# Perceiver attention block on one core: scores in four row tiles of 32 partitions instead of two of 64, with three rotating PSUM banks instead of five

## What is computed

```
x = x + xattn(layernorm(x), ctx)    # x [8, 64, 256]; ctx [8, 1601, 256]; 16 heads of 16
x = x + causal self attention(layernorm(x))
x = x + top-2 of 8 experts(layernorm(x))             # 256 -> 1024 -> 256, exact gelu

xattn:  k = ctx @ Wk.T + bk;  v = ctx @ Wv.T + bv;  q = norm @ Wq.T + bq
        attn = softmax(q . k / 4)                     # per head, over the 1601 keys
        out  = (attn @ v) @ Wo.T + bo
```

## Time and profile before

| | us |
|---|---|
| median of 3 runs | 750.23 (747.94 to 752.42) |
| the profiled execution | 751.15 |
| its span | 749.1 |
| PE busy / DVE busy / ACT busy / POOL busy | 683.8 / 499.6 / 326.5 / 224.6 |
| matmul instructions | 6584 |
| granted TensorE clock, mean | 0.949 |

### The profile page before, as it was taken

The page is one execution under the profiler, slowest core; times in us unless marked ns, Lnnn a source line. Parts: engine busy times, 40 slices in busy tenths (PEclk is TensorE's granted clock), DMA queues, the critical chain, the costliest instruction groups (busy, mean ns, idle before and its releaser), DMA issues.

```text
span 749.1 us, 16666 instructions
## 1 busy us (share of the span) xinstructions
PE 683.8 (91%) x6584; PEld 551.7 (74%) x6584; DVE 499.6 (67%) x868; ACT 326.5 (44%) x517; POOL 224.6 (30%) x111
## 2 busy tenths in 40 slices
PE   2979999999999977999997999978787999999997
PEld 2657877778867855886775787656666999999996
DVE  4783697796658773666768657476466766766753
ACT  2434465554454542445454443345225544444431
POOL 1004566665445542535454545200000000000000
PEclk9987999999999986999998999897798999999999
DMA  6120020010010110001001000020500222112000
GB/s 221 59 67 2 23 67 24 24 46 23 24 46 4 40 49 3 24 24 45 3 23 45 1 2 2 1 114 1 225 1 1 113 113 112 32 83 112 0 0 28
DMA packets 12501, 34.16 MB, mean 46 GB/s; under 512 B 1483, under 2 KB 9812, under 8 KB 10260
## 3 DMA queue, kind: packets, MB, share of 16 engines
q1 hardware_dynamic: 12180, 31.62, 12.4%
q0 software_dynamic: 256, 1.58, 0.6%
HBM read 32.67 MB, written 0.52 MB: 44 GB/s over the span
## 4 chain that ended last, share of the span: by engine, by line
PE 79%; DVE 13%; issue 3%; ACT 2%; DMA 1%; SPq 0%; DVEq 0%; POOL 0%; ACTq 0%
PE bank L1016 44%; PE bank L1180 13%; PE bank L1025 8%; PE bank L1076 5%; DVE maxes L763 3%; DVE ctx_lo L704 2%; PE bank L1119 2%; PE bank L1110 2%; DMA bias_sb<-in_biases 1%; PE bank L1094 1%; ACT probs L639 1%; DVE qbd_hi L736 1%; DVE prob_sum L431 1%; DVE ties L811 1%; DVE shift L722 1%
## 5 line engine op out<-in xcount | busy, mean ns | idle before, releaser
L431 POOL TENSOR_TENSOR prob_sum<-probs,prob_sum 128x1024 f32<-128x1024 f32 x84 | 201.8, 2402 | 162.6 <-ACT probs L639 161.6
L763 DVE TENSOR_REDUCE maxes<-bank 128x1 f32<-128x400 f32 (+1 forms) x256 | 132.5, 567 | 33.2 <-PE bank L1076 30.6
L639 ACT ACTIVATE probs<-bank 128x1024 f32<-128x1024 f32 (+1 forms) x104 | 106.6, 1025 | 98.0 <-PE bank L1180 94.8
L621 ACT ACTIVATE h_raw<-bank,b_sb 128x512 f32<-128x512 f32 (+1 forms) x72 | 46.2, 642 | 105.6 <-PE bank L1016 105.6
L544 ACT ACTIVATE v_sb<-bank 128x256 f32<-128x256 f32 (+1 forms) x104 | 39.9, 384 | 104.5 <-PE bank L1016 104.2
L745 DVE SCALAR_TENSOR_TENSOR k_lo<-bank,bias_sb,k_hi 128x400 fp32r<-128x400 f32 (+2 forms) x64 | 40.6, 634 | 62.0 <-ACT k_hi L541 61.9
L1180 PE MATMUL bank<-qbd_hi,k_hi 64*128 64x256 f32 (+1 forms) x416 | 74.3, 352 | 6.7 <-ACT probs L639 3.4
L1016 PE MATMUL bank<-w_hi,h_hi 128*128 128x256 f32 x256 | 72.7, 284 | 0.2 <-DVE h_lo L963 0.2
L1016 PE MATMUL bank<-w_hi,h_lo 128*128 128x256 f32 x256 | 72.5, 283 | 0.0
L1025 PE MATMUL bank<-probs,v_sb 128*32 128x128 f32 (+1 forms) x1664 | 70.1, 288 | 2.5 <-DVE masked L712 2.0
L1016 PE MATMUL bank<-w_lo,h_hi 128*128 128x256 f32 x256 | 72.3, 283 | 0.0
(11 more groups left out here) (157 smaller groups left out, 1474.2 us busy)
## 6 DMA issues: line engine op xcount, KB each, us to landing
raw<-in_w SPq DMA_DIRECT2D x16, 1024.0 KB, 6.7
ctx_raw<-in_ctx_t SPq DMA_DIRECT2D x16, 400.0 KB, 3.5
ctx_raw<-in_ctx_t SPq DMA_DIRECT2D x8, 402.0 KB, 3.6
ctx_raw<-in_ctx_t SPq DMA_DIRECT2D x8, 399.0 KB, 3.5
w_sb<-in_w_t POOLq DMA_DIRECT2D x1, 1280.0 KB, 10.4
x_all<-in_x SPq DMA_DIRECT2D x1, 512.0 KB, 3.7
w_raw<-in_w_t SPq DMA_DIRECT2D x1, 512.0 KB, 4.7
result<-x_all SPq DMA_DIRECT2D x1, 512.0 KB, 2.7
```

Of the source, the lines that this page charges most:

```text
L431: engine.tensor_tensor(prob_sum[0:ROWS[k], :], probs[0:ROWS[k], s % 2, :], acc[0:ROWS[k]], ALU.add).then_inc(summed, 1)
L621: nc.scalar.activation(h_raw[:, c % 2, 0:width], bank[:, at, 0:width], ACT.Gelu, bias=b1_sb[:, bass.ds(e, 1), c:c + 1].rearrange("p a b -> ...
L639: nc.scalar.activation(probs[0:ROWS[k], s % 2, :].rearrange("p (g n) -> p g n", g=G), bank[0:ROWS[k], 0:ROW_TILES, :], ACT.Exp, scale=SCAL ...
L763: nc.vector.tensor_reduce(maxes[:, g * PAIRS + j, c:c + 1], src[:, 0:width], AX.X, ALU.max).then_inc(read_dve, 1)
```

## The change

Four row tiles of 32 partitions take the place of two of 64. A row tile holds two heads, so `qbd` has 2 x 64 = 128 columns per group, half of before, and its mask is the two-column parity mask that was already loaded. Each row tile writes to its own bank, so scores take four banks (256 columns of each), and the ring of units keeps three. The M units, still taken two at a time, contract over 32 partitions. The order of probabilities in `probs` changes with it, and its size does not.

```
-ROW_TILES = 2
+ROW_TILES = PAIRS
 RT = P // ROW_TILES
 RH = HG // ROW_TILES
+M_AT_ONCE = 2
...
-RING = 5
+RING = 3
...
     c, rest = divmod(u, G * PAIRS)
-    g, rest = divmod(rest, PAIRS)
-    i, r = divmod(rest, ROW_TILES)
+    g, j = divmod(rest, PAIRS)
...
-                                         bank[0:ROWS[k], 0:ROW_TILES, :], ACT.Exp,
+                                         bank[0:ROWS[k], 0:ROW_TILES, 0:G * RH * Q], ACT.Exp,
...
-                mask = row_mask[:, :].unsqueeze(1).unsqueeze(3).broadcast_to([P, G, RH, Q])
+                mask = mask_sb[:, HG:HG + RH].unsqueeze(1).unsqueeze(3).broadcast_to([P, G, RH, Q])
...
-                r, i = divmod(j, PAIRS // ROW_TILES)
-                return (r * G + g) * (PAIRS // ROW_TILES) + i
+                return j * G + g
...
-                    rows = slice(RT * r, RT * r + RT)
+                    rows = slice(RT * j, RT * j + RT)
                     ins = nc.tensor.matmul(dst[:, 0:width],
-                                           qbd_hi[rows, parity, g, 2 * i:2 * i + 2, :].rearrange("p s q -> p (s q)"),
+                                           qbd_hi[rows, parity, g].rearrange("p s q -> p (s q)"),
```

More of the change, by code:

```diff
@@ L67, in in_order @@
             for k in counts}
-M_PAIRS = K_UNITS * PAIRS // ROW_TILES
+M_PAIRS = K_UNITS * PAIRS // M_AT_ONCE
 M_AT = in_order({1: 2, 2: 1, 3: 2, 4: 1, 5: 2, 6: 2, 7: 1, 8: 2, 9: 2, 10: 1})
@@ L99, in both_tiles @@
 def both_tiles(pairs):
-    return [("M", ROW_TILES * u + r) for u in pairs for r in range(ROW_TILES)]
+    return [("M", M_AT_ONCE * u + r) for u in pairs for r in range(M_AT_ONCE)]
 READ_BY_ACT = {"v", "V", "VL", "X", "xt1", "qk", "st00", "st01", "st10", "st11", "xt2", "router", "gt"}
@@ L192, in step_units @@
     row = m + others
-    ahead = len(m[:ROW_TILES])
+    ahead = len(m[:M_AT_ONCE])
     row += [("VL", KT - 1)] if own and k == LAST_V_AT else []
@@ L202, in unit_of_max @@
     c, rest = divmod(u, G * PAIRS)
-    g, rest = divmod(rest, PAIRS)
-    i, r = divmod(rest, ROW_TILES)
+    g, j = divmod(rest, PAIRS)
     width = EDGE[c + 1] - EDGE[c]
-    return c, g, r * (PAIRS // ROW_TILES) + i, width + width % 2
+    return c, g, j, width + width % 2
 def add(a, b, times=1):
@@ L258, in perceiver_kernel @@
         mask_sb = sb("mask_sb", [P, HG + 2])
-        row_mask = sb("row_mask", [P, RH])
         bias_sb = sb("bias_sb", [P, 3, DC])
@@ L638, in tile @@
                         act.wait_ge(summed, n - 1)
-                    nc.scalar.activation(probs[0:ROWS[k], s % 2, :].rearrange("p (g n) -> p g n", g=G),
-                                         bank[0:ROWS[k], 0:ROW_TILES, :], ACT.Exp,
+                    nc.scalar.activation(probs[0:ROWS[k], s % 2, :].rearrange("p (r n) -> p r n", r=ROW_TILES),
+                                         bank[0:ROWS[k], 0:ROW_TILES, 0:G * RH * Q], ACT.Exp,
                                          scale=SCALE).then_inc(exp_done, 1)
@@ L878, in _ @@
             dve.wait_ge(weights_in, 48)
-            link(nc.vector.tensor_tensor(row_mask[:, :], mask_sb[:, 0:RH], mask_sb[:, RH:HG], ALU.add))
             dve.wait_ge(q_split, G)
```

## The result

The changed kernel takes 793.72 us (median of 4 runs, 790.78 to 796.86), the kernel before 749.09 (743.16 to 752.42) beside it. The ratio is 1.0606 with a 95% interval of 1.0526 to 1.0686: slower, as forecast, but by 45 us where the forecast had 16, and just outside the range. The profiled execution took 790.78 us with a span of 788.8. Medians in this document are over all executions of a kernel, while the ratios leave out those more than 1.5% above its fastest, such as one of 931.89 us among the four with the altered table of M units.

The account below looks back on a forecast made before the run. PE, busy 91% of the span, was taken as the bound. Losses of 31.8 us less gains of 19.2 gave +12.6; with 3 for the clock, 751.15 became 766.8, forecast as 766, range 744 to 792 for 8 in 10.

Parts of the forecast that it names:

- Scores: Score slots on PE, bound by weight loads: 0.14 us saved per full step, 17.2 us together with last steps.
- rivals A: Four row tiles load and multiply side by side, a slot takes 0.06 us: 8 us faster, 743; chance 18%.
- B: Narrow score slots take longer than wide ones, 0.24 us each: far slower, 833 us; chance 9%.
- Where PE waits: PE waits for late readings with three banks: prologue 6.4 us, second steps 11.1, ninth steps 8.7.
- Regular steps: Steps with four M units: K waits 0.06 us and the saved 0.14 is lost; 1.7 and 3.9 us in all.
- DVE: Spreading fewer query columns gains DVE some 9 us, but only 2.0 us on PE's path, at first M units.
- D: A late PE gives DVE time to catch up, ring costs under half: 750 to 740 us; chance 4%.
- the clock: New PE pauses add perhaps a tenth to 77 us at the lower clock: 3 us lost, bounds 0 and 12.
- Rival C: Late DVE at batch boundaries and the clock amplify each other, both terms double: 780 to 800 us; chance 9%.

Follow-up runs that it names:

- altered table of M units: Changed kernel, one pair of M units fewer in second and ninth steps, one more in third and eleventh: 773.43 us; on the kernel before: 740.85 us.
- ring-alone kernel: The kernel before, still with two row tiles, with its ring of banks cut from five to three: 792.74 us, ratio 1.0609.
- ring of four: The kernel before with its ring of banks cut from five to four: 762.73 us, ratio 1.0220.
- DVE's order: The changed kernel, DVE reading the M units filled ahead of the second step's scores before the last batch's division: 779.25 us, ratio 1.0435.
- all three remedies: The changed kernel with a five-bank ring in the prologue, the altered table of M units and DVE's order: 772.84 us, ratio 1.0318.

## Why the prediction was wrong

The direction and the waits were right. The size was off by one term, the clock, and a gain that no term had hid part of the error.

- **Scores.** Right. Load-bound slots were forecast to save 0.14 us a step, and a step saves 0.17 (the step with 65 keys 0.35 in batches 2 and 4, where the forecast had 0.48); rivals A (0.06 us a slot) and B (0.24) are out, since both would show in the regular step.
- **Where PE waits.** Right in all three kinds of place, and by the size of a wait at full clock: 1.80 us against 1.85 in the second step of the ring-alone kernel; 2.09 in the ninth step of batch 2. The ninth steps of batches 0 and 1 went from 2.99 to 4.10, 1.1 against 1.0. PE's idle time for `maxes` and `k_lo`, 24 us, is of the size of the 27.9 forecast.
- **Regular steps.** Right: the 0.14 saved is waited away in those with four M units, which went from about 4.28 to 4.37.
- **DVE.** Its busy time fell by 9.7 us, forecast 9. But the wait of the first M unit for the queries, which was to go (minus 2.0), is still 1.6.
- **D** (a late PE lets DVE catch up) is out at the batch boundaries, where the six second steps lost 18.7 us. What it describes did happen at the gates, which it did not name: two pauses of 4.68 us went.
- **The failed step is the clock.** The prediction added "3, between bounds of 0 and 12" for it, from the reasoning that new pauses "may add a tenth" to 77 us at the lower level. They added 96 us, and the table's remainder, 39.7 - 12.6 = 27 us, is nine times the term. With the 12.3 us gained at the gates in it, what the forecast missed is nearer 39, under the 46 that the estimate from the busy times allows the clock. That the clock is behind much of it was shown by filling the pauses: 18 us came back though the waits for DVE's readings got no shorter and those for the gates grew by 9.5. The ring-alone kernel agrees: its waits were forecast at 27.9 us (6.4 + 11.1 + 8.7 + 1.7), it lost 44.9, and it stood 31 us longer at half clock, which can cost up to half of that, 15.5, if work at 1.2 GHz takes twice as long. In the ring of four the half clock did not grow, and the loss was 13.6. Rival C named the pair (waits and clock amplify each other) and its 780 to 800 holds the result, but it doubled both terms; the waits had their forecast size, and the clock term was at least nine times too small.

The reasoning error can be seen in the trace of before. I took it that pauses of 1 to 2 us would each cost a piece in proportion to their length. But the dips of the earlier trace rows stand behind pauses of 1.7 to 4.7 us, and two of these are under 2: behind one of 1.70 us PE stood at 1.2 GHz for 6.8 us, behind one of 1.95 for 10.2. The first of them, and the window behind it:

```profile
466.69 3.03 PE L1110 MATMUL bank<-k_t,qbd 128*128 128x64 f32 x16 [1.70 <-issue]
...
467.40:474.20 6.80, 6.80 (x50) 5.72 (x48) 4.08 (x6) 0.38 (x1) 1.39 (x1) 0.50 0.01 2
```

Not every pause does it: one of 1.99 us at 489.6 has no dip behind it. In the trace after, a pause of 1.47 us is followed by 3.4 us at 1.2 GHz, and one of 2.09 by 17.1 us. The upper bound of 12 was no bound: nothing in the rows limited the time at half clock to a small multiple of the pauses. The Trainium skill ("TensorE: Matmul & The Clock Gate", A second HAM failure mode: psum-queue depth-cycling) tells of just this: a kernel that cycles through PSUM banks pauses briefly and often, and swings between the two clock levels. The trace agrees with it (79 us at the lower level before, 175 after), and it should have been a rival of its own.

What stays open: how the lost time divides exactly between clock and waits, since 18 us is what the filling gave back net of its own work and of the longer waits for the gates; how much of the gain of the altered table is the ring's, as it also gave 8 us with five banks; why a stretch lasts 3.4 us at one place and 17 or 44 at another; and why removing one pause moves the stretch instead of shortening it, as in the runs with DVE's order and with all three remedies.

## What to carry to other kernels

Before giving up PSUM banks on a PE-bound kernel, list each place where the unit a ring-length back is read later than PE would start, and price the pause and then the clock behind it: here 28 us of waits were forecast and at least 27 us came on top. List the long waits elsewhere as well, since a late engine can hide in them: two pauses of 4.7 us went, and came back when more of the time was at full clock. Narrower row tiles save little when each slot loads its own weights; compare the load's time with the matmul's before counting the columns. If a pause cannot be removed, idle matmuls in it can pay, as twelve of 1.48 us did in a pause of 1.47; in steps at full clock without a pause six of them cost 0.9 us.

## What the runs showed of the hardware

- Time went down by 18 us when 12 and 8 useless matmuls of 256 bf16 columns were added to steps in which PE waited; 12 of them took 1.48 us.
- Weight loads of 32 partitions by 128 f32 columns last about as long (216 ns) as those of 64 (202). Four go in side by side, the next four 0.10 to 0.11 us later, and this bounds a slot of four row tiles near 0.1 us.
- Ring lengths of 5, 4 and 3 on the same code gave 1, 1.022 and 1.061: the second bank costs about twice the first (1.8 times by the ratios, 2.3 by the medians), and only with it does the half clock grow (79, 74, 110 us).
- PE was busy for 35.39 of 37.20 us and stayed at 1.2 GHz, so a high busy share does not mean a high clock: read both lines of the page together.
- The same kernel took 741.1 to 744.5 us in executions with a granted clock of 0.957 to 0.964, and 745.0 to 751.0 with 0.946 to 0.955.
- Pauses of 1.47, 1.70, 1.95 and 2.09 us were followed by 3.4, 6.8, 10.2 and 17.1 us at 1.2 GHz, one of 1.99 us by none.
